# Attention and a block-quantised linear layer on one core: one shared addition masks the diagonal banks, and a transposing transfer turns the maxima

## The reference, cut to what matters

```
x = x + attention(layernorm(x))          # x: 4 x 2048 x 256, float32
x = x + mx_linear(layernorm(x))          # both operands quantised in blocks of 32

def attention(x):                        # 16 heads of 16 channels, causal
    q, k, v = x @ Wq, x @ Wk, x @ Wv
    scores = where(causal, q @ k.T, -inf)
    ctx = softmax(scores / sqrt(256)) @ v
    return ctx @ Wo + bo
```

## Time and profile before

| | |
|---|---|
| time, median of 3 runs | 2093.06 us (2091.07 to 2094.66) |
| profiled execution, its own time | 2085.36 us |
| its span, first to last instruction | 2083.6 us |
| PE busy | 1980.0 us, 95% |
| DVE busy | 1716.6 us, 82% |
| ACT busy | 1351.9 us, 65% |
| POOL busy | 810.7 us, 39% |
| mean granted TensorE clock | 0.987 |

### The profile page before, as it was taken

The page is one execution under the profiler, slowest core; times in us unless marked ns, Lnnn a source line. Parts: engine busy times, 40 slices in busy tenths (PEclk is TensorE's granted clock), DMA queues, the critical chain, the costliest instruction groups (busy, mean ns, idle before and its releaser), DMA issues.

```text
span 2083.6 us, 35416 instructions
## 1 busy us (share of the span) xinstructions
PE 1980.0 (95%) x11749; PEld 755.4 (36%) x11749; DVE 1716.6 (82%) x4358; ACT 1351.9 (65%) x2881; POOL 810.7 (39%) x1123
## 2 busy tenths in 40 slices
PE   6799899999999999999999999999999999999984
PEld 3333333333333343434334343433333433333433
DVE  4797886869887978796897879797889899888875
ACT  5357566767766767676766666666766666677661
POOL 3323414231335554553243646453345444211232
PEclk9999999999999999999999999999999999999997
DMA  4442221414041241703323161340614121130000
GB/s 155 123 111 64 77 68 38 102 48 120 9 123 55 74 99 38 174 11 81 93 53 95 46 140 50 79 102 17 160 39 112 54 55 40 39 90 24 9 31 21
DMA packets 162963, 152.04 MB, mean 73 GB/s; under 512 B 32982, under 2 KB 150492, under 8 KB 162780
## 3 DMA queue, kind: packets, MB, share of 16 engines
q1 hardware_dynamic: 162780, 149.77, 27.0%
HBM read 91.89 MB, written 57.02 MB: 71 GB/s over the span
## 4 chain that ended last, share of the span: by engine, by line
PE 71%; DVE 19%; ACT 3%; issue 3%; POOL 2%; SPq 2%; DMA 1%; POOLq 0%; ACTq 0%; DVEq 0%
PE psum L1496 20%; PE psum L1479 19%; PE psum L1464 16%; DVE max_parts L1201 8%; PE psum L1560 8%; PE psum L1553 5%; DVE psum L1196 4%; ACT probs L1005 2%; SPq L674 1%; PE psum L1531 1%; DVE max_parts L1196 1%; ACT acc_sb L1014 1%; PE psum L1582 1%; PE psum L1523 1%; DVE stats L1259 1%
## 5 line engine op out<-in xcount | busy, mean ns | idle before, releaser
L1005 ACT ACTIVATE probs<-psum 128x512 f32<-128x512 f32 (+3 forms) x2560 | 1211.6, 536 | 518.9 <-PE psum L1479 511.8
L1201 DVE TENSOR_REDUCE max_parts<-psum 128x1 f32<-128x512 f32 x1536 | 965.2, 682 | 123.6 <-PE psum L1464 119.5
L1479 PE MATMUL psum<-q_rows,k_rows 99*128 99x512 bf16 (+3 forms) x2560 | 856.1, 351 | 3.3 <-ACT probs L1005 1.9
L1464 PE MATMUL psum<-k_rows,q_rows 96*128 96x512 bf16 (+3 forms) x2560 | 815.7, 349 | 30.2 <-DVE max_parts L1201 11.4
L1496 PE MATMUL psum<-probs,v_in 128*17 128x512 f32 (+3 forms) x5120 | 594.3, 536 | 11.9 <-ACT acc_sb L1014 11.5
L1196 DVE CUSTOM_DVE_ANT_0 psum<-psum,causal 128x128 f32<-128x128 f32 (+3 forms) x1024 | 476.5, 518 | 135.5 <-PE psum L1464 132.7
L1479 PEld LDWEIGHTS psum<-q_rows,k_rows 99*128 99x128 bf16 x2560 | 237.2, 97 | 640.5 <-ACT probs L1005 500.3
L833 POOL TENSOR_SCALAR_AFFINE_SELECT probs<-probs 128x512 f32<-128x512 f32 x256 | 165.9, 648 | 727.3 <-ACT probs L1005 727.1
L1464 PEld LDWEIGHTS psum<-k_rows,q_rows 96*128 96x128 bf16 x2560 | 244.6, 98 | 291.7 <-DVE max_parts L1201 81.8
L1496 PEld LDWEIGHTS psum<-probs,v_in 128*17 128x17 f32 x5120 | 86.1, 95 | 226.7 <-issue 162.1
L1196 DVE DVE_READ_ACCUMULATOR2_ANT max_parts<- 128x1 f32 x1024 | 144.9, 141 | 0.0
(11 more groups left out here) (161 smaller groups left out, 1268.7 us busy)
## 6 DMA issues: line engine op xcount, KB each, us to landing
q_rows<-qk_scratch SPq DMA_DIRECT2D x384, 64.0 KB, 2.7
k_rows<-qk_scratch SPq DMA_DIRECT2D x384, 64.0 KB, 2.7
qk_scratch<-shop SPq DMA_DIRECT2D x56, 384.0 KB, 3.2
sums_scratch<-acc_sb SPq DMA_DIRECT2D x48, 256.0 KB, 2.3
shop<-in_L_attn_x SPq DMA_DIRECT2D x19, 512.0 KB, 5.2
v_scratch<-shop SPq DMA_DIRECT2D x16, 544.0 KB, 4.3
v_in<-v_scratch SPq DMA_DIRECT2D x64, 136.0 KB, 2.6
out_shop<-in_L_attn_x SPq DMA_DIRECT2D x12, 512.0 KB, 8.5
```

Source lines behind the costliest of these rows:

```text
L1005: nc.scalar.activation(probs[s % NPROBS][:, h, a:CHUNK], bank[SCORE_BANKS[n % 3]][:, a:CHUNK], ACT.Exp, scale=SCALE).then_inc(probs_ready, 1)
L1201: nc.vector.tensor_reduce(max_parts[k % 2][:, first:first + heads, t % TILES, c], ring_bank(UNIT_USE[n])[:, 0:heads * width] .rearrange("p ...
L1464: ins = nc.tensor.matmul(dst[:, i * width:(i + 1) * width], q_rows[u][0:ROWS, qc, first + i, t % TILES * P:(t % TILES + 1) * P], k_rows[u] ...
L1479: nc.tensor.matmul(bank[SCORE_BANKS[n % 3]][:, a:CHUNK], k_rows[u][0:ROWS + LEVELS, h, kb * P:(kb + 1) * P], q_rows[u][0:ROWS + LEVELS, qc ...
```

## The change

It has two parts.

**Diagonal banks.** Where a diagonal bank holds more than one head, one addition on DVE adds the 128 x 128 triangle of the mask to the last 128 columns of every head in the bank at once. DVE then waits for it (`link`), and the instruction of the off-diagonal units reduces all heads of the bank. Banks with one head keep the fused instruction.

**Maxima.** PE's `turn_max` and ACT's `take_turned_max` are gone, and with them one use of the ring per piece. In their place SP issues one transposing transfer from `neg_wide` (`neg_max` widened to 128 x 128 bfloat16) to `max_rows`, one slot after POOL's split. `load_max` stands one slot later, as it did, and waits for the landing (`max_turned`).

```diff
 for k in range(NK):
     p = vector(MAX_DONE[k], 0.3, "maximum", k)
     p = pool(p + 1, 0.9, "split_max", k)
-    p = item(p + 1, 0.15, "turn_max", k)
-    sync(p + 1, "load_max", k)
+    sync(p + 1, "turn_max", k)
+    sync(p + 2, "load_max", k)
...
+            def turn_max(k):
+                sp.wait_ge(neg_ready, k + 1)
+                wait(sp, row_loaded[k % 2], 48 * (k // 2))
+                sp.dma_start_transpose(max_rows[k % 2][:, None, :], neg_wide[k % 2][:, :]).then_inc(max_turned, 16)
+
             def load_max(k):
                 g, qc = divmod(k, QC)
-                sp.wait_ge(scalar_emptied, ITEM_NO["turn_max", k])
+                sp.wait_ge(max_turned, 16 * (k + 1))
...
             def take_unit(n):
...
+                if c == QCS[k] and heads == 1:
+                    mine = ring_bank(UNIT_USE[n])[:, 0:width]
+                    nc.vector.tensor_tensor_reduce(
+                        out=mine, in0=mine, in1=causal[:, CHUNK - width:CHUNK], scale=1.0, scalar=LOWEST, op0=ALU.add,
+                        op1=ALU.max, accum_out=max_parts[k % 2][:, first, t % TILES, c:c + 1]).then_inc(unit_used, 1)
+                    return
                 if c == QCS[k]:
-                    if n == 0:
-                        dve.wait_ge(consts_ready, 1)
-                    for i in range(heads):
-                        mine = ring_bank(UNIT_USE[n])[:, i * width:(i + 1) * width]
-                        ins = nc.vector.tensor_tensor_reduce(
-                            out=mine, in0=mine, in1=causal[:, CHUNK - width:CHUNK], scale=1.0, scalar=LOWEST, op0=ALU.add, op1=ALU.max,
-                            accum_out=max_parts[k % 2][:, first + i, t % TILES, c:c + 1])
-                    ins.then_inc(unit_used, 1)
-                    return
+
+                    mine = ring_bank(UNIT_USE[n])[:, 0:heads * width].rearrange("p (h n) -> p h n", h=heads)
+                    mine = mine[:, :, width - P:width]
+                    triangle = causal[:, None, CHUNK - P:CHUNK].broadcast_to([P, heads, P])
+                    link(nc.vector.tensor_tensor(out=mine, in0=mine, in1=triangle, op=ALU.add))
                 nc.vector.tensor_reduce(max_parts[k % 2][:, first:first + heads, t % TILES, c],
...
-            def turn_max(k):
-                pe.wait_ge(neg_ready, k + 1)
-                use = ITEM_USE["turn_max", k]
-                emptied(pe, use)
-                nc.tensor.transpose(ring_bank(use)[0:LEVELS * HG * TILES, :].bitcast(BF16)[:, 0:P],
-                                    neg_max[k % 2][:, :, :].rearrange("p l n -> p (l n)"), identb[:, :]
-                                    ).then_inc(for_scalar, 1)
```

More of the change, by code:

```diff
@@ L436, in layer_kernel @@
         ident = sbuf("ident", [P])
-        identb = sbuf("identb", [P], BF16)
         causal = sbuf("causal", [CHUNK])
@@ L462, in layer_kernel @@
         neg_rest = [sbuf(f"neg_rest{u}", [HG * TILES]) for u in range(2)]
-        neg_max = [sbuf(f"neg_max{u}", [LEVELS, HG * TILES], BF16) for u in range(2)]
+        neg_wide = [sbuf(f"neg_max{u}", [P], BF16) for u in range(2)]
+        neg_max = [t[:, 0:LEVELS * HG * TILES].rearrange("p (l n) -> p l n", l=LEVELS) for t in neg_wide]
         max_rows = [sbuf(f"max_rows{u}", [P], BF16) for u in range(2)]
@@ L556, in layer_kernel @@
         v_loaded = [[sem(f"v_loaded{u}_{c}") for c in range(QC)] for u in range(2)]
+        max_turned = sem("max_turned")
         row_loaded = [sem(f"row_loaded{u}") for u in range(2)]
@@ L771, in _ @@
             for p in SLOTS:
+                for k, in at("turn_max", p):
+                    turn_max(k)
                 for k, in at("load_max", p):
@@ L806, in _ @@
         def _(pool):
-            nc.gpsimd.memset(ident[:, :], 0.0)
             nc.gpsimd.memset(causal[:, :], 0.0)
             nc.gpsimd.memset(half_power[:, :], -0.5)
-            nc.gpsimd.memset(identb[:, :], 0.0).then_inc(const_step, 1)
+            for u in range(2):
+                nc.gpsimd.memset(neg_wide[u][:, :], 0.0)
+            nc.gpsimd.memset(ident[:, :], 0.0).then_inc(const_step, 1)
             pool.wait_ge(const_step, 1)
-            for m in (ident, identb):
-                nc.gpsimd.affine_select(out=m[:, :], in_=m[:, :], compare_op=ALU.not_equal, fill=1.0, base=0,
-                                        pattern=[[-1, P]], channel_multiplier=1)
+            nc.gpsimd.affine_select(out=ident[:, :], in_=ident[:, :], compare_op=ALU.not_equal, fill=1.0, base=0,
+                                    pattern=[[-1, P]], channel_multiplier=1)
             triangle = causal[:, CHUNK - P:CHUNK]
@@ L1014, in copy_acc @@
                 nc.scalar.copy(acc_sb[k % 2][:, :], acc_bank).then_inc(acc_copied, 1)
[L1016 to L1021, removed]
             def take_turned_x(n, e):
@@ L1060, in take_items @@
             def take_items(p):
-                for k, in at("turn_max", p):
-                    take_turned_max(k)
                 for n, e in at("turn_x", p):
@@ L1606, in items @@
             def items(p):
-                for k, in at("turn_max", p):
-                    turn_max(k)
                 for k, in at("turn_acc", p):
```

10 lines of the change are left out of this document (6 added, 4 removed).

## The result

The change makes the kernel slower: the ratio to the kernel before is 1.0068, 95% interval 1.0053 to 1.0083. The median after is 2106.61 us. The profiled execution took 2101.6 us. Its own distance to the one before (2085.36) is 16, but single executions differ by several us, so sizes are taken from the ratios.

The account below looks back on a forecast made before the run. PE was taken to bound most of the span, DVE about a fifth. -10.7 (PE) + 13 (DVE) + 1.8 (piece 63) = +4.1, plus 1 for the prologue: +5 us, 2098 us; range 2081 to 2119.

Parts of the forecast that it names:

- DVE's extra occupancy: Multi-head diagonal banks: 0.36 us more per four-head bank, 0.30 per two-head bank, 61 us over 64 pieces.
- Rival 4: DVE's multi-head banks: durations add up after all, so 40 us less on DVE; -18 us, 2075 us; chance 0.06.
- 0.22 x 61 = 13 us: DVE's extra time reaching the path, at the 22% of L1196's busy time on the chain; bounds 0 and 61.
- Rival 3: DVE following shorter PE: half of the 61 us on the path, PE's ring waits doubled; +21, 2114 us; chance 0.10.
- -10.7 + 1.8 = -8.9: PE's turn: 41 transposes on the chain at 0.26 us gained, less 1.8 us of delay at piece 63.
- PE without its transposes, some 15 us less busy: Sign in the profile after: PE's busy time falls some 15 us once its 64 transposes are gone.
- T: Time from `neg_ready` to landing of the turned maxima: 2.7 us, bounds 1.6 and 9.2, delaying only piece 63.
- with nothing behind it that is due in those slots: SP's queue: let go 1.4 us later at piece 27, delaying nothing due there; cost taken as 0.
- Rival 2: SP's transposing transfer is slow, 5 us up: 2107 us at 5, 2151 us at 9.2; chance 0.16.
- the prediction's sum over the pieces: PE's delays from late maxima, added over tight pieces: 10.6 us at a transfer time of 5, 55 at 9.2.
- 1 us of allowance: Prologue: SP's queue, itself on the chain, holds two more waits ahead of the row loads; 1 us added.

Follow-up runs that it names:

- the mask alone: Kernel before with the shared addition and plain reduction in all multi-head diagonal banks, turn still by PE and ACT: +21.1 us.
- idle-operation kernels: Kernel before plus 192 unread DVE operations on SBUF, ahead of multi-head banks or of single-head banks: ratio 1.0213, +44.5 us each.
- the turn alone: Kernel before with the transposing transfer replacing the turn by PE and ACT, fused maxima kept: 2083.26 us, -8.4 us.
- the doubled transpose: Kernel before with a second, unread TensorE transpose behind each of the 64 turns: ratio 1.0013, +2.7 us.
- the doubled transfer: The turn alone with a second transposing transfer started when the first has landed: ratio 1.0067 to the kernel before, 22 us more than the turn alone.
- the unmasked one: Kernel before with the causal mask left out of the maxima, every diagonal bank one plain reduction: ratio 0.9940, -12.5 us.

## Why the prediction was right, and where not

The forecast was +5 us and 2098 us; the kernel took +14.2 us and 2106.61. Direction and range hold, the size is short by 9 us.

- **DVE's extra occupancy: right.** 1.34 us was found for the four-head bank (1.32 predicted). For the two-head bank the spacings give 1.06 (1.055), where nothing else holds the next bank. Busy time is 1766.3 (about 1767). The bound from one overlapping timeline carried, and L1241 was a fair price for an addition with the mask broadcast over the heads (692 ns, measured 697). Rival 4, that durations add up, is out: the mask alone would have been a gain. By the Trainium skill (VectorE: DVE Perf Modes, section The DRAIN you can't avoid) a semaphore between operations costs nothing extra, so the wait between addition and reduction would be free. The trace disagrees: 0.73 us from start to start with the wait, 0.61 without. The prediction left out that the same section says that an operation that is not held starts earlier; with that sentence the 0.61 against a duration of 0.69 agrees.
- **How much of it is on the path: the step that failed.** "I take the same share, 0.22 x 61 = 13 us." The mask alone measured 21.1 us [18.4, 24.0], 0.35 of the 61, where the prediction took 0.22. That is 8 of the 9 us that are missing. The share of a chain is an average over what is there now. Here it came close to what DVE's time was worth when some was taken away (0.20 measured), and not to what more of it cost. The prices measured are 0.20 per us of busy time going down, 0.40 going up by 20 to 51 us in three kernels that fill the time by an addition and a reduction, and 0.40 in one that reads the bank again. Rival 3 had the mechanism, "PE is now shorter and DVE follows it closer", but with a half and for the wrong reason: the mask alone, with PE no shorter, already costs it. That the banks come back later and PE's ring waits grow is in the rows; that the price rises with the load, and that the 0.51 to 0.67 of the idle-operation kernels belong to the same curve, is only argued. Ring waits did not double, as rival 3 would have had them: 109.8 us before, 152.0 after.
- **PE's gain: the size is right, its working only in part.** -10.7 + 1.8 = -8.9 was forecast for the turn with its transfer, -8.4 [-11.3, -5.4] measured. The sign named for it failed: "PE without its transposes, some 15 us less busy" was to be seen in the profile after, and there PE is 1.1 us busier than before (1981.1 and 1980.0). It is 15.0 us less busy than in the mask alone, but only 7.8 less in the turn alone than before (1972.2), and 20.1 less with the maxima unmasked in both (1981.1 and 1961.0). Busy times of PE from single executions scatter by several us. And the doubled transpose shows that only 0.07 of the 0.26 us is the transpose's own passage.
- **The transfer: right for the maxima, wrong in one term put at 0.** For T 2.7 us was taken, 2.26 came. One wait at piece 63, 1.16 us long against 0.32 before (predicted 1.8 more, measured 0.8), and none elsewhere in this profile; the turn alone has three, 2.2 us in all. But SP's two waits per piece were put at 0, "with nothing behind it that is due in those slots". That was read at one piece. DVE's waits for `den` and for the input of the layer norm were 0.2 and 5.4 us before and are 3.2 and 6.7 after, 4.3 us more, and PE stands behind the longest one for `den` (2.47 us, then 3.08 on PE). Rival 2 didn't come true, but it was priced too low: the prediction's sum over the pieces gives some 7 us at T = 4.5, and the doubled transfer cost 22. It left out what queues behind the transfer.
- **Prologue.** The 1 us of allowance was neither confirmed nor refuted. The first scores start at 94.1 us before and 93.1 after, but between 93.1 and 97.6 over all kernels, with and without the transfer.
- **The clock.** In the profiled executions the mean granted clock is 0.981 after against 0.987 before, but that one execution before was high: over its runs the kernel before has 0.983, the kernel after 0.980. Within one kernel the executions with the lower clock are the longer ones: with the mask in four-head banks only, the six at 0.985 or 0.986 took 2094.2 to 2096.0 us, the four at 0.980 to 0.982 took 2097.4 to 2103.8. In the 23 runs of the kernel before beside the last experiments it is 1.3 us per 0.001. By that, an estimate, 0.003 would be some 4 of the 14 us, and 0.002 of the mask alone 2 to 3 of its 21. Whether the lower clock is a cause of its own or follows from PE's longer waits is open. It doesn't order the kernels: the turn alone and the unmasked one have 0.983, as before, and are faster, and the idle operations in single-head banks have 0.983 and are 44.5 us slower.

## What to carry to other kernels

Merging several small instructions into two that wait for each other can load an engine more. Price it by start-to-start times, not by durations or counts. Where two engines hand banks to each other, the share of the chain may price only time that you take away: here it did, and time that was added cost about twice as much. Test with an experiment that only adds time of the same kind. A transfer that the issuing queue waits for also delays what stands behind it; look for its effect on the engines that wait for those loads, not only on its own result. And ask whether the work is needed: not masking at all beat both ways of masking, by 12.5 us, and with the transposing transfer by 21.9.

## What the runs showed of the hardware

The transposing transfer of 128 x 128 bfloat16 lands 2.2 us after its issue in the median, 0.5 us later than a plain load of the rows, and SP is busy with its issue for 1.12 us against 0.59. The two issues after:

```profile
L696 SPq DMA_DIRECT2D q_rows<-max_rows x192: 513/589/1837, 70.3 to 1995.1; - x192
L689 SPq DMA_TRANSPOSE max_rows<-neg_max x64: 1108/1124/1950, 67.8 to 1991.6; - x64
...
DMA to landing us min/median/max: 2.2/2.2/8.6
```

The Trainium skill (VectorE: DVE Perf Modes, section The three transpose paths) gives 1.31 us for it. Here even the fastest took 2.2, from issue to landing.

It also moves the data in small pieces. The page's packets after:

```profile
DMA packets 173197, 154.09 MB, mean 73 GB/s; under 512 B 43222, under 2 KB 160732, under 8 KB 173020
```

Before there were 162963 packets, 32982 of them under 512 B: some 10,000 more small packets for 64 transfers, 160 each. Their cost in time doesn't show in any run.
